# Seven of seventeen edge tiles multiplied whole in the neighbour sums, and longer buffer rings beside them

## The reference

```python
x: (6250, 512); src, dst: (100000,), sorted by dst; D = 512, 8 experts, top 2

def _sage_layer(h, src, dst, W_self, W_neigh, b, n_nodes):
    agg = jax.ops.segment_sum(h[src], dst, num_segments=n_nodes)
    deg = jax.ops.segment_sum(jnp.ones_like(dst, dtype=h.dtype), dst, num_segments=n_nodes)
    h_neigh = agg / jnp.maximum(deg, 1.0)[:, None]
    return jax.nn.relu(h @ W_self + h_neigh @ W_neigh + b)

h = layernorm(x)
h = _sage_layer(h, src, dst, W_self1, W_neigh1, b1, N)
h = _sage_layer(h, src, dst, W_self2, W_neigh2, b2, N)
x = x + h
x = x + moe(layernorm(x))     # logits, top 2 of 8 experts, relu FFN, layer norm per expert
```

## Time and profile before

| what | value |
|---|---|
| median of 3 runs | 3018.88 us (3018.03 to 3023.58) |
| the profiled execution's own time | 3014.28 us |
| its span, first to last instruction | 3012.5 us |
| mean granted TensorE clock | 0.956 of 2.4 GHz |
| first layer's gathers (L678, x782) | 97 to 1144 us |
| second layer's gathers (L678, x782) | 1167 to 2218 us |
| experts | 2262 to 3012 us |

### The profile page before, as it was taken

How to read it: one execution, slowest core, us unless ns; L and a number is a source line. 1 busy time by engine, 2 the same in 40 slices (tenths; PEclk the granted TensorE clock), 3 DMA queues, 4 the chain that set the end, 5 groups by cost and what they waited for, 6 DMA issues and landing times.

```text
span 3012.5 us, 64212 instructions
## 1 busy us (share of the span) xinstructions
PE 2692.1 (89%) x11698; PEld 1974.8 (66%) x11699; DVE 2024.5 (67%) x4826; ACT 1455.0 (48%) x2703; POOL 2091.6 (69%) x2213
## 2 busy tenths in 40 slices
PE   1499999999999997999999999999978999999996
PEld 0376666676766664666666666666656778777875
DVE  6566666666655554777777777777775667666765
ACT  4454544454444443444444444444434555555554
POOL 0577777777777775777777777777734656666665
PEclk9999999999999998999999999999988999999998
DMA  8689898989887776787778787777755554555444
GB/s 323 222 271 293 294 294 290 293 293 299 288 256 222 227 220 214 243 251 241 241 245 247 242 248 244 244 243 244 240 189 147 139 138 99 118 140 139 82 77 67
DMA packets 234481, 663.25 MB, mean 220 GB/s; under 512 B 46512, under 2 KB 48106, under 8 KB 227264
## 3 DMA queue, kind: packets, MB, share of 16 engines
q0 software_dynamic: 151472, 464.79, 55.2%
q10 hardware_dynamic: 62260, 128.09, 12.0%
q1 hardware_dynamic: 20700, 69.89, 6.2%
HBM read 550.93 MB, written 111.69 MB: 220 GB/s over the span
## 4 chain that ended last, share of the span: by engine, by line
POOL 40%; issue 21%; DMA 19%; PE 14%; DVE 2%; SPq 1%; POOLq 1%; ACT 1%; ACTq 1%; DVEq 1%
POOL store_all L678 36%; DMA m_g<-gate_scratch,idx_g 6%; PE ps L1609 5%; DMA store_all<-h_scratch,srcT 4%; DMA out<-store_all,idx_s 3%; PE ps L1635 3%; DMA store_all<-xn_scratch,srcT 2%; PE ps L1644 2%; POOL idx_x L691 2%; PE ps L1645 2%; DMA xn_scratch<-store_all 1%; DMA store_all<-xn_scratch,idx_x 1%; SPq L366 1%; POOL store_all L707 1%; DMA store_all<-in_x 1%
## 5 line engine op out<-in xcount | busy, mean ns | idle before, releaser
L823 ACT ACTIVATE r_hi<-store_all 128x512 fp32r x1190 | 731.6, 627 | 680.4 <-SPq L562 470.7
L1216 DVE TENSOR_TENSOR r_lo<-store_all,r_hi 128x512 fp32r<-128x512 f32 x1190 | 808.8, 687 | 289.7 <-ACT r_hi L823 288.0
L678 POOL DMA_INDIRECT store_all<-h_scratch,srcT x782 | 812.4, 1039 | 261.1 <-issue 220.0
L678 POOL DMA_INDIRECT store_all<-xn_scratch,srcT x782 | 808.8, 1034 | 238.5 <-issue 231.2
L1644 PE MATMUL ps<-r_hi,sel 128*128 128x512 f32 x1190 | 574.7, 483 | 50.6 <-DVE r_lo L1216 50.5
L1635 PE MATMUL ps<-store_all,sel 128*128 x980 | 533.6, 627 | 0.0
L1645 PE MATMUL ps<-r_lo,sel 128*128 128x512 f32 x1190 | 484.3, 407 | 0.0
L1204 DVE TENSOR_TENSOR sel<-ps,dstT 128x384 fp32r (+4 forms) x602 | 315.9, 525 | 200.3 <-PE ps L1635 120.5
L1609 PE MATMUL ps<-wts,sT 128*128 128x512 f32 x1176 | 411.5, 461 | 0.0
L1609 PE MATMUL ps<-wts,aT 128*128 128x512 f32 x1176 | 374.4, 427 | 0.0
L1609 PE MATMUL ps<-wts,m_hT 128*128 x1224 | 322.4, 414 | 19.1 <-DVE m_hT L1489 18.1
(11 more groups left out here) (274 smaller groups left out, 3325.8 us busy)
## 6 DMA issues: line engine op xcount, KB each, us to landing
expert_weights_scratch<-w_both ACTq DMA_DIRECT2D x64, 512.0 KB
wts<-expert_weights_scratch SPq DMA_DIRECT2D x32, 1024.0 KB, 9.4
store_all<-in_L_ffn_W ACTq DMA_DIRECT2D x64, 256.0 KB
self_t<-xn_scratch ACTq DMA_DIRECT2D x49, 256.0 KB
self_t<-h_scratch ACTq DMA_DIRECT2D x49, 256.0 KB
store_all<-in_x ACTq DMA_DIRECT2D x49, 256.0 KB
store_all<-xn_scratch,srcT POOLq DMA_INDIRECT x782, 4.4
store_all<-h_scratch,srcT POOLq DMA_INDIRECT x782, 4.1
```

What stands on the lines that cost most here:

```text
L678: pool.indirect_dma_start(rows[:, t % SLOTS, :], None, rows_d, bass.IndirectOffsetOnAxis(ap=srcT[:, t:t + 1], axis=0)).then_inc(s_rows[t % ...
L823: act.activation(r_hi[:, ring(k), :], slot_of(t), ACT.Copy) \
L1216: dve.tensor_tensor(r_lo[:, ring(k), :], slot_of(t), r_hi[:, ring(k), :].bitcast(F32), ALU.subtract).then_inc(S["lo"] if k < ST else S["lo ...
```

## The change

Seven tiles of a group go whole, 2, 5, 7, 9, 11, 13 and 15, where it was five, 2, 5, 8, 11 and 14; ten are split where it was twelve. The places of `r_hi` and `r_lo` are now counted over split tiles alone (`ring` goes by `split_no(k) % 6`), so that whole tiles take none. `sel` gets nine places (`SRING`) and its own rule (`sel_ring`). `free_at` is worked out from the tiles that use the same place.

```diff
-WHOLE = (2, 5, 8, 11, 14)
+WHOLE = (2, 5, 7, 9, 11, 13, 15)
+SRING = 9
...
-            sel = sbc(c2, "sel", [P, RING, P], F32R)
+            sel = sbc(c2, "sel", [P, SRING, P], F32R)
...
         def ring(k):
-            return k % RING if k < ST else RING - 1
+            return split_no(k) % RING if k < ST else RING - 1
+        def sel_ring(k):
+            return k % SRING if k < ST else SRING - 1
-        def free_at(g, k):
-            if k == ST:
-                return g * ST + (ST // RING * RING + RING)
-            if k >= RING:
-                return g * ST + (k + 1)
-            return g * ST + (RING + min(k - (ST % RING - 1), 0))
+        def free_at(g, k, at):
+            users = [u for u in range(ST) if at(u) == at(k) and (at is sel_ring or u not in WHOLE)]
+            ahead = [u for u in users if u < k]
+            last = ahead[-1] if ahead else users[-1] - ST
+            return g * ST + max(RING + last + 1, 0)
...
-                    act.wait_ge(S["seg"], free_at(g, k))
+                    act.wait_ge(S["seg"], free_at(g, k, ring))
...
-                        a = ring(k)
-                        dve.wait_ge(S["seg"], free_at(g, k + w - 1 if k < ST else ST))
+                        a = sel_ring(k)
+                        dve.wait_ge(S["seg"], max(free_at(0, k + i, sel_ring) for i in range(w)) + g * ST)
...
-                    a = ring(k)
+                    a, r = sel_ring(k), ring(k)
...
-                    pe.matmul(agg_of(g), sel[:, a, :], r_hi[:, a, :], start=k == 0, stop=False)
-                    pe.matmul(agg_of(g), sel[:, a, :], r_lo[:, a, :], start=False, stop=False) \
+                    pe.matmul(agg_of(g), sel[:, a, :], r_hi[:, r, :], start=k == 0, stop=False)
+                    pe.matmul(agg_of(g), sel[:, a, :], r_lo[:, r, :], start=False, stop=False) \
```

More of the change, by code:

```diff
@@ L475, in of_half, with ring @@
                 t[:, bass.ds(q % 2, 1), :].rearrange("p a d -> p (a d)")
-        def ring(k):
-            return k % RING if k < ST else RING - 1
         def split_no(k):
             return k - len([w for w in WHOLE if w < k])
-        def free_at(g, k):
-            if k == ST:
-                return g * ST + (ST // RING * RING + RING)
-            if k >= RING:
-                return g * ST + (k + 1)
-            return g * ST + (RING + min(k - (ST % RING - 1), 0))
+        def ring(k):
+            return split_no(k) % RING if k < ST else RING - 1
[6 more added lines that the diff above has]
+            return g * ST + max(RING + last + 1, 0)
         def slot_of(t):
```

## The result

The changed kernel takes 3065.6 us (3057.91 to 3070.05, 4 runs) against 3018.45 us (4 runs): 1.0144 times as long, with a 95% interval of 1.0127 to 1.0161. That is 47 us, where 42 were forecast. The profiled execution took 3063.36 us, 49 us above that of before.

What follows compares the result with a forecast made beforehand. POOL's gathers were taken to set the pace, with PE becoming slower in the second layer after the change. First layer -11, second layer +51, its first groups +2 gave +42 us, 3061 us; range 3026 to 3079 us.

Steps and rivals of the forecast that it cites:

- PE's need: Both layers: each added whole tile costs PE 0.40 us, making 19.8 us a group in the first, 21.2 in the second.
- Who is the bound: First layer: POOL stays the bound, PE just below; second layer: PE with its falls becomes slower and `freed` holds POOL.
- The boundary's gaps: Group boundary, second layer: PE's waits of 0.34 and 0.86 us both stay, 1.2 us in all.
- The falls of the clock: Second layer: 20 ordinary boundaries followed by a PE clock fall, where 8 were, at 1.6 us each, 32 us.
- my 12 to 30: Second layer: range of ordinary boundaries followed by a fall counted as the forecast, 3048 to 3077 us, chance 0.62.
- my +51: Second layer's 46 windows between group ends: 1044 us forecast against 993 before.
- the clock keeps its habit: Rival, second layer: still 8 falls at ordinary boundaries, 1025 us there, +23 in all (3042 us); chance 0.14.
- neither way to a faster kernel: Rivals: all clock falls go (3003 us), or the boundary's 1.2 us vanish (2997 us); chance 0.10 together.
- POOL's gain: Gathers: each r_lo costs POOL 0.114 us, so 98 fewer a layer give 11 us less POOL time a layer.
- a gather mean that stays at 1.034: Sign against the forecast, in the first layer's gathers: it would mean the POOL term is 0.
- The first layer's end: First layer: PE stays just below POOL's pace and the layer gets 11 us shorter.
- Behind the layers: Stretch behind the second layer: forecast to change by 0 us.

Runs made afterwards that it cites:

- old7: Kernel before with seven whole tiles and nothing else changed (old buffer places): 3544.7 us, 1.0046 on a slower chip.
- whole3: Changed kernel with three whole tiles (2, 8, 14) in place of seven: 3563.0 us, 1.0019, and 3553.1 us, 0.9986, on slower chips.
- late7_again: Changed kernel with DVE's residual moved behind the r_lo of tile 16: 3053.2 us, 1.0108; the earlier run, on a slower chip, 3588.2 us, 1.0093.
- pad3: Changed kernel with five whole tiles as before and three r_lo products a group issued twice: 3577.5 us, 1.0057, and 3581.9 us, 1.0070, on slower chips.
- late5: Kernel before with DVE's residual moved behind the r_lo of tile 16: 3538.9 us, 0.9936 on a slower chip.
- second7: Changed kernel with five whole tiles in the first layer, seven in the second: 3571.1 us, 1.010; again 3613.1 us, 1.0202, on slower chips.

## Why the prediction was right, and where it wasn't

**PE's need: right.** 0.40 us a whole tile, 19.8 and 21.2 us a group. After has both to within 0.1 us. `old7` bears it out on another chip, and `whole3` to 0.2 us (18.39 and 19.6 us for the 18.2 and 19.6 that the same price gives). It carries 46 x 0.8 = 37 us of the second layer.

**Who is the bound: right.** POOL is held for slots in pieces up to 4.7 us, and the second layer's length is PE's.

**The boundary's gaps: right.** 0.34 and 0.89 us.

**The falls of the clock: mis-sized.** This is the term that the second layer's forecast had wrong. I put n = 20 ordinary boundaries with a fall behind them; there are 11 (8 ordinary windows of 22.7 and 22.8 us and three long ones at 0.93), just outside my 12 to 30. Reading the windows from one to the next shows which half of the argument failed. Behind a window without a fall, 10 of 23 ordinary boundaries brought one, which is the "about one in two" of the prediction. Behind a window with a fall, 1 of 15 did, where I took the same one in two; before, 6 of 7 had fallen behind the slow windows at 0.86. At the new pace a fall is nearly always followed by a group without one. With the long groups' followers at 24.5 rather than 25.0 us, the sum by the prediction's own terms becomes

- 46 x 21.2 = 975.2
- long groups 7 x 1.6 = 11.2
- falls at ordinary boundaries 11 x 1.6 = 17.6
- behind the long groups 6 x 3.3 + 1.9 = 21.7
- the first two windows 1.5 + 0.4 = 1.9

together 1027.6 us, where 1027.4 was measured and 1044 foreseen. The sum had another flaw, which was small. By the same terms the windows of before make 46 x 20.4 + 10.5 + 26.6 + 8 x 1.6 = 988 us, and 993.3 were measured; the other 5 us are windows in which PE waited, such as 22.60 and 20.90 us at the start of the layer. I set a sum without such windows against a measurement with them, so my +51 was 5 us low by its own terms. After has 1.9 us of them. The rival "the clock keeps its habit" (8 falls, 1025 us) was nearer for this layer. The boundary's gaps didn't vanish, and all 7 long groups were again followed by a fall, so neither way to a faster kernel came about. The rule of the Trainium skill that led there (TensorE: Matmul & The Clock Gate, section "What's actually happening", throttled is the default and activity releases it) doesn't decide here: PE was busy for 966 of 1027 us (0.940) against 927 of 993 (0.933), and the falls became no fewer, 18 for 15.

**POOL's gain: wrong, in kind.** I took 0.114 us for each `r_lo`, 11 us a layer, from a mean and from an instance in which "an `r_lo` started within" the gather. The rows of before around that instance show a better reading:

```profile
605.11 0.69 DVE L1216 TENSOR_TENSOR r_lo<-store_all,r_hi 128x512 fp32r<-128x512 f32 x1 [0.40 <-ACT r_hi L823]
...
606.92 0.95 POOL L678 DMA_INDIRECT store_all<-xn_scratch,srcT  x1 [0.30 <-issue]
607.38 0.68 DVE L1216 TENSOR_TENSOR r_lo<-store_all,r_hi 128x512 fp32r<-128x512 f32 x1
```

The gather of 1.38 us began at 605.24, while an `r_lo` was already running (605.11 to 605.80). The next, at 606.92, had an `r_lo` start within it, at 607.38, and took 0.95. So did the one at 608.17, which I had taken for a gather without any: an `r_lo` starts at 608.76.

Sorted over all gathers of both traces, by the last `r_lo` that began ahead of the gather:

- begun less than 0.30 us earlier: 1.28 to 1.32 us on average in the four gather stages
- 0.30 to 0.45 us earlier: 1.12 to 1.14 us
- 0.45 us earlier or more, or none: 0.96 to 0.97 us, also where an `r_lo` starts within the gather

The exceptions to the last line are 11 gathers in the second layer of after, 1.67 to 1.76 us long. They began during a short one-hot build of DVE (L1368), and an `r_lo` started 0.17 to 0.26 us later.

A sign that I had named myself, a gather mean that stays at 1.034, had come too (1.039).

So what counts is the phase. It is also the kind of instruction. Of 458 gathers that began less than 0.30 us after a selection build, `sT`, `aT` or `residual`, which have one input in PSUM (`ps`), none took over 0.96 us. Those that began so behind DVE's `r_lo` or the same subtraction on wider weight tiles, with both inputs in SBUF, took 1.30 us on average (518) and 1.67 us (15, 128x1024). In the first layer most gathers above 1.2 us that the list above doesn't explain began while DVE worked on these weight tiles (17 of 19 in before, 15 of 17 in after).

In the first layer of before a gather began less than 0.45 us behind an `r_lo` 177 times, with 591 `r_lo` in the stage, after it 176 times with 494, and the time above 0.95 us was 65.9 and 69.6 us. The removed steps were not those that collided. In the second layer there were 229 and 144, and it fell from 69.5 to 58.6 us, where POOL no longer decides. That an overlap makes the gather longer is read from the traces; no kernel without `r_lo` was run.

By the Trainium skill (SBUF — State Buffer, section "Who interferes with whom") a tensor_tensor was seen not to stall descriptor generation. That would have given the right value for the sum, 0, though the traces disagree with its reason.

**The first layer's end: missed.** The layer took 7 us more. The gathers have 3.8 us of it, about what their time above 0.95 us grew by (3.7). The other 3.5 us lie between the last gather and the last group's end, 8.8 us before and 12.3 after. PE is busy there without a gap:

```profile
1147.10:1159.40 12.30, 12.30 (x54) 8.45 (x53) 3.86 (x8) 2.97 (x5) 0.00 (x0) 1.00 0.16 56
```

I had written that PE stays just below POOL. On average it does, but groups with a fall put it behind, and with 0.8 us less room a group it still had 3.5 us more to do when POOL had finished. `late7_again` has the same first layer: its gathers take 1045.4 us and the last group ends 12.3 us behind them, 1057.7 in all. So the 3.5 us came again and the 3.8 us didn't. The slower chips bear out the 3.5. There the stretch from the last gather to the last group's end is 28.4 and 28.6 us with three whole tiles in the first layer, 30.0 in four traces with five, 31.6 in three with seven, and 31.1 and 31.4 in the two `pad3`, with the old places (`late5`, `old7`) as with the new. So this stretch goes by PE's work.

**Behind the layers: not foreseen, not explained.** 8 us more, in code that was not touched. Over all the traces this stretch took 782.3 to 797.2 us. The kernel before is at the low end, but `late7`, with seven whole tiles and the new places, took the same 782.3 us, and `second7` and `second7_again`, one kernel, took 791.5 and 797.2. So it may well be the execution and not the change. PE's share of the 8 us is 3 us of busy time (712.2 against 709.2); the rest is waiting.

So 3061 against 3065.6 us is partly luck. From the forecast's 42 us to the 49 of the profiled executions it is -17 for the 46 windows, nearly all of it the falls, -2 for the first groups of the second layer, +11 for POOL's gain, +7 for the first layer and +8 for what stands behind.

## What to carry to other kernels

Price PE work by start-to-start distances and read the loop's need from the shortest windows of whole iterations: this held to 0.1 us in the second layer's trace on the first chip, and in the first layer in all traces with five and seven whole tiles. When two engines share a loop with one microsecond of room, moving work to the nearly full one cost almost its whole price here (34 of 39 us), and relief on engines that already wait gave nothing back. Before putting a slowdown down to the number of neighbours, sort its instances by what was running when they began; if the phase decides, taking a sixth of the neighbours away can change nothing. Before adding up terms for the changed kernel, add up the same terms for the old one and compare the sum with its measured time.

## What the runs showed of the hardware that I had not expected

- The same kernel took 3018 us on one chip and 3536 to 3558 us on others, 17 to 18% more, nearly all of it in the two layers. In the trace of `late5` from such a chip ACT and DVE stand 3 to 7 us, again and again, for no engine of the kernel.
- An indirect gather on POOL takes 0.95 us, also with an fp32 subtraction (two SBUF inputs, 0.69 us) starting within it, and 1.28 to 1.32 us on average when one started less than 0.30 us before it. Behind a DVE instruction of the same length with one input in PSUM (`sT`, `aT`) it takes 0.95 us in every case.
- PE's gap of 0.86 us at the bias matmul, put down to "issue", is not a fixed cost of the loop. In the second layer it is longer than 0.5 us at 44 boundaries of after, and at only 7 of `late7_again`, those behind long groups, where PE still waits for the extra tile. So it seems to follow a wait of PE for DVE some 2 us earlier. Why it should, no run shows.
